# Vision block on one core: variances and gate logit in four 32-column tiles, roots and gate weights spread through DRAM

## What is computed

```python
h = tokens(x, W, b)                        # 196 patches + class token
h = h + attention(layernorm(h))            # 16 heads, "stablemax3" in place of softmax
h = h + experts(layernorm(h))

# layernorm: (x - mean) / sqrt(var + 1e-5) over the 256 channels of a token
# experts, per token:
u = sigmoid(x @ Wu + bu)                   # the gate logit, one number a token
k = clip(ceil(4 * u), 1, 4)
h = relu(x @ W1[e] + b1[e]);  y[e] = h @ W2[e] + b2[e]
out = sum over i = 1..4 of where(k >= i, u / i, 0) * y[(token + i - 1) % 4]
```

## Time and profile before

| | |
|---|---|
| median of 3 runs | 3939.52 us (3939.36 to 3940.41) |
| span of the profiled execution | 3943.7 us; this is all the time that the profile has for it |
| PE busy | 3883.3 us (98%), 30276 records |
| PE weight loads (beside PE) | 3412.1 us (87%) |
| DVE, POOL, ACT busy | 2816.3 (71%), 2819.3 (71%), 2380.1 us (60%) |
| DMA | 545.57 MB, mean 138 GB/s; SP's queue 46.7% of 16 engines |
| chain that ended last | PE 95% |

### The profile page before, as it was taken

How to read it: one execution, slowest core, us unless ns; L and a number is a source line. 1 busy time by engine, 2 the same in 40 slices (tenths; PEclk the granted TensorE clock), 3 DMA queues, 4 the chain that set the end, 5 groups by cost and what they waited for, 6 DMA issues and landing times.

```text
span 3943.7 us, 87143 instructions
## 1 busy us (share of the span) xinstructions
PE 3883.3 (98%) x30276; PEld 3412.1 (87%) x30276; DVE 2816.3 (71%) x4315; ACT 2380.1 (60%) x4388; POOL 2819.3 (71%) x3543
## 2 busy tenths in 40 slices
PE   7899999999999999999999999999999999999998
PEld 4688888888888888888888888888888888888887
DVE  5767777777777677777777777777777777777753
ACT  5655566655666655666555666556665556665552
POOL 5666777767777667777677776677776777766676
PEclk8999999999999999999999999999999999999999
DMA  7244444444444444444444444444444444444455
GB/s 237 91 138 142 123 145 140 134 139 139 127 142 137 141 139 126 141 140 134 141 137 129 144 136 139 137 129 138 142 135 143 136 129 141 137 138 125 136 148 140
DMA packets 776547, 545.57 MB, mean 138 GB/s; under 512 B 157624, under 2 KB 701752, under 8 KB 775096
## 3 DMA queue, kind: packets, MB, share of 16 engines
q1 hardware_dynamic: 771416, 539.70, 46.7%
q10 hardware_dynamic: 4704, 0.30, 0.1%
HBM read 518.48 MB, written 21.30 MB: 137 GB/s over the span
## 4 chain that ended last, share of the span: by engine, by line
PE 95%; POOL 1%; ACT 1%; DVE 1%; issue 1%; DMA 0%; ACTq 0%; SPq 0%; POOLq 0%; DVEq 0%
PE ps L1336 66%; PE ps L1420 5%; PE ps L1435 5%; PE ps L1449 5%; PE ps L1534 4%; PE ps L1543 3%; PE ps L1551 2%; PE ps L1518 1%; PE ps L1512 1%; PE ps L1332 1%; PE ps L1524 1%; PE ps L1500 1%; PE ps L1506 1%; ACT probs L712 0%; DVE lows L1046 0%
## 5 line engine op out<-in xcount | busy, mean ns | idle before, releaser
L1336 PE MATMUL ps<-xn,w1s 128*128 128x197 f32 x4096 | 910.1, 343 | 4.6 <-ACT hT L677 2.3
L1336 PEld LDWEIGHTS ps<-xn,w1s 128*128 128x128 f32 x4096 | 676.6, 189 | 144.0 <-issue 132.3
L1336 PE MATMUL ps<-hT,w_s 128*128 128x197 f32 x4064 | 783.8, 330 | 7.6 <-issue 7.3
L971 DVE SCALAR_TENSOR_TENSOR probs<-probs,ps 99x788 f32<-99x788 f32 x512 | 483.4, 970 | 323.4 <-ACT probs L712 323.4
L1336 PEld LDWEIGHTS ps<-hT,w_s 128*128 128x128 f32 x4064 | 691.7, 190 | 9.6 <-issue 7.9
L568 POOL TENSOR_TENSOR hT<-hT 128x197 f32<-128x197 f32 x508 | 331.4, 652 | 511.9 <-ACT hT L692 508.7
L1336 PE MATMUL ps<-xt,w1s 128*128 128x197 f32 x3072 | 681.8, 330 | 3.3 <-ACT hT L683 1.7
L561 POOL TENSOR_SCALAR hT<-hT 128x394 f32<-128x394 f32 x512 | 642.7, 1255 | 19.2 <-DVE hT L1092 19.2
L1046 DVE TENSOR_REDUCE lows<-ps 99x8 f32<-99x1576 f32 (+1 forms) x256 | 460.3, 1799 | 219.4 <-PE ps L1435 219.4
L1336 PE MATMUL ps<-hT,w_a 128*128 128x197 f32 x3048 | 591.0, 329 | 0.2 <-DVE yw L1110 0.2
L1336 PEld LDWEIGHTS ps<-xt,w1s 128*128 128x128 f32 x3072 | 539.1, 190 | 36.3 <-DVE hT L1098 3.4
(11 more groups left out here) (142 smaller groups left out, 6231.8 us busy)
## 6 DMA issues: line engine op xcount, KB each, us to landing
w_s<-w_sums SPq DMA_DIRECT2D x508, 256.0 KB, 3.6
w_a<-in_w SPq DMA_DIRECT2D x384, 256.0 KB, 3.3
w1s<-w_sums SPq DMA_DIRECT2D x512, 192.0 KB, 2.6
w1s<-in_w SPq DMA_DIRECT2D x512, 128.0 KB, 2.3
x<-in_xT SPq DMA_DIRECT2D x30, 1188.0 KB, 7.3
w1s<-in_w SPq DMA_DIRECT2D x512, 64.0 KB, 1.9
w1s<-w_sums SPq DMA_DIRECT2D x512, 64.0 KB, 1.9
out_rows<-rows SPq DMA_DIRECT2D x252, 48.0 KB
```

The source lines that it names most:

```text
L971: nc.vector.scalar_tensor_tensor(out=part, in0=part, scalar=3.75, in1=ps[0:HB, 2 * half:2 * half + 2, 0:N], op0=ALU.add, op1=ALU.mult).the ...
L1336: return mm(place, weights, rows, start=start, stop=True, skip_group_check=True)
```

## The change

`variance`, `variance2` and the gate logit are computed in four products each, with 32 weight columns and 100 of the tokens (QUARTERS starts at 0, 100, 197 and 297), each into its own 32 partitions of one bank. A partition group so holds a quarter of the tokens, and eps, roots, Newton step, sigmoid and gate weights are worked on 128 x 100 instead of 128 x 394. To have them on all partitions again, SP stores one partition of each group (4 x 100) to DRAM, waits, and reads it back to all 128 partitions: `spread_rstd`, `spread_rstd2` (200 KB read) and `spread_weights` (four experts, 800 KB read). The logit is summed from hc instead of xn2, inside `variance2`, and is multiplied by the root afterwards; `gate_product` and `gate_sum` move ahead, `gates` moves from s = 5 to s = 3, the variance of f half a unit later and into bank Y1.

```diff
+        QUARTERS = (0, QW, S, S + QW)
...
+            def spread_rstd(f):
+
+                sp.wait_ge(rstd_ready, at(f, 1, 1))
+                wait(sp, xn2_ready, at(f - 2, 1, 1))
+                sp.dma_start(rstd_rows, rstd_q[0:P:32, :]).then_inc(rstd_out, 16)
+                sp.wait_ge(rstd_out, at(f, 16, 16))
+                sp.dma_start(rstd[:], rstd_rows.rearrange("q x -> (q x)").partition_broadcast(P)).then_inc(rstd_in, 16)
...
+            def spread_weights(n):
+
+                sp.wait_ge(gate, at(n, GATES, GATES))
+                wait(sp, yw_ready, 2 * n * E)
+                sp.dma_start(weight_rows.rearrange("e q x -> q e x"), w_q[0:P:32, 0:E * QW].rearrange("q (e x) -> q e x", e=E)).then_inc(we_out, 16)
+                sp.wait_ge(we_out, at(n, 16, 16))
+                sp.dma_start(w_e[:], weight_rows.rearrange("e q x -> (e q x)").partition_broadcast(P)).then_inc(we_in, 16)
...
                 for s in range(16):
+                    if s == 4 and has_f and f > 1:
+                        spread_rstd(f)
+                    if s == 15 and has_b:
+                        spread_rstd2(b, has_f)
+                    if s == 5 and has_n:
+                        spread_weights(n)
...
             def gates(n):
 
-                pool.wait_ge(gate, at(n, 9, 3))
-                wait(pool, yw_ready, 2 * n * E)
+                pool.wait_ge(gate, at(n, GATES, 2))
+                wait(pool, we_in, at(n, 16, 0))
...
-                    if s == 5 and has_n:
+                    if s == 3 and has_n:
                         gates(n)
...
             def normal_rows2(b):
-                refine_1(b, rs2_ready, nt2_ready, ht2_ready)
-                refine_2(b, ht2_ready, rstd2_ready)
-                nc.vector.tensor_tensor(xn2[:, b % 2], hc[:], rstd[:].unsqueeze(1).broadcast_to((P, DK, N)), ALU.mult).then_inc(xn2_ready, 1)
+                dve.wait_ge(rstd2_in, at(b, 16, 16))
+                for kk in range(DK):
+                    ins = nc.vector.tensor_tensor(two(xn2[:, b % 2, kk, :]), two(hc[:, kk, :]), padded(rstd[:]), ALU.mult)
+                ins.then_inc(xn2_ready, 1)
...
-                mm(bank("var2", b)[:, 0:N], mean_w[:], xn2[:, b % 2, 0, :], start=True, stop=True).then_inc(var2_done, 1)
-
-            def gate_logit(b, *free):
+                squared = xn2[:, b % 2].rearrange("p k n -> p (k n)")
+                for i, first in enumerate(QUARTERS):
+                    ins = mm(quarters(i)[:, home("var2", b), 0:QW], mean_w[:, 32 * i:32 * i + 32], squared[:, first:first + QW], start=True, stop=True)
+                ins.then_inc(var2_done, 1)
                 pe.wait_ge(zs_ready, at(b, 1, 1))
-                for w in free:
-                    pe.wait_ge(*w)
-                mm(bank("z", b)[:, 0:N], ones[:], hc[:, 0, :], start=True, stop=True).then_inc(z_done, 1)
+                for i, first in enumerate(QUARTERS):
+                    ins = mm(quarters(i)[:, home("var2", b), QW:2 * QW], ones[:, 32 * i:32 * i + 32], zs[:, first:first + QW], start=True, stop=True)
+                ins.then_inc(z_done, 1)
```

More of the change, by code:

```diff
@@ L46, in vit_block @@
     GP = 200
+    QW = GP // 2
     UNITS = E * FB
@@ L96, in vit_block @@
         carrier = sb("carrier", [P, 1])
[L97 to L100, removed]
+        zs = sb("zs", [P, 2 * GP])
+        zb = sb("zb", [P, QW])
+        ez = sb("ez", [P, QW])
+        u = sb("u", [P, QW])
+        w_q = sb("w_q", [P, E * (QW + 1)])
+        w_e = sb("w_e", [P, E * 2 * GP])
         hT = sb("hT", [P, (RING * 2 + RING2 * 2 + RINGT * 3) * S])
@@ L467, in _ @@
                 nc.gpsimd.memset(tile[:], 1.0).then_inc(pool_const, 1)
-            for tile in (xn, q_max, k_one, lows, h2, zb):
+            for tile in (xn, q_max, k_one, lows, h2, zb, zs):
                 nc.gpsimd.memset(tile[:], 0.0).then_inc(pool_const, 1)
@@ L796, in ez_of @@
                 act.wait_ge(zb_ready, at(n, 1, 1))
-                wait(act, gate, at(n - 1, 9, 9))
+                wait(act, gate, at(n, GATES, 0))
                 nc.scalar.activation(ez[:], zb[:], ACT.Exp, scale=-1.0).then_inc(ez_ready, 1)
@@ L1115, in y_weighted @@
                     dve.wait_ge(d2_ready, x + 1)
-                    dve.wait_ge(gate, at(x // E, 9, 9))
+                    dve.wait_ge(we_in, at(x // E, 16, 16))
                 else:
@@ L1252, in step @@
                         odd_up(k)
+                    if k == 3 and has_f:
+                        refine_2(f, ht_ready, rstd_ready)
                     if has_b:
@@ L1291, in step @@
                     even(8 + k)
+                    if k == 7 and has_b:
+                        normal_rows2(b)
+                    if k == 6 and has_b:
+                        refine_1(b, rs2_ready, nt2_ready, ht2_ready)
+                        refine_2(b, ht2_ready, rstd2_ready)
                     if has_f:
                         low(f, k)
+                    if k == 6 and has_b:
+                        zb_of(b)
                     odd_up(8 + k)
@@ L1312, in step @@
                     if k == 5 and has_b:
+                        gate_sum(b)
+                        logits(b)
                         spread(b, "var2", var2_done, vt2_ready)
-                    if k == 6 and has_b:
-                        normal_rows2(b)
-                        gate_sum(b)
-                    if k == 7 and has_b:
-                        zb_of(b)
                     if k == 7 and has_f:
@@ L1684, in step @@
                 experts(1)
+                experts(1)
                 if has_f:
-                    variance(f, read(5))
-                experts(1)
+                    variance(f, (h_ready, at(f, 2, 2)))
                 if has_b:
-                    gap(b, 3, read(6), *([(vt_ready, at(f, 1, 1))] if has_f else []))
+                    gap(b, 3, read(6))
                 experts(1)
@@ L1694, in step @@
                 if has_b:
-                    weigh(b, 0)
+                    weigh(b, 0, *([(vt_ready, at(f, 1, 1))] if has_f else []))
                     gap(b, 4, read(8))
```

125 lines of the change are left out of this document (77 added, 48 removed).

## The result

The changed kernel takes **4080.8 us** (median of 4 runs, 4072.18 to 4088.23) against 3939.44 us: 1.0355 times as long, 95% interval 1.0342 to 1.0367. The prediction was 4005 with a range up to 4055. The sign was right; the size was 76 us short.

What follows compares the result with a forecast made beforehand. TensorE (PE) was taken as the bound, busy 120.38 of 120.42 us a step. Steady terms of +1.1 a step gave +33 us, the start +33: +66, median 4005 us, chance 0.50, range up to 4055.

Steps and rivals of the forecast that it cites:

- What PE saves: On PE, 0.35 us from the variance and 0.73 from variance 2 with logit: 1.1 a step, -33 us in all.
- Rival (c): On PE, the tiles do not run side by side: +0.5 a step in place of -1.1, 4053 us; chance 0.04.
- The variance moves half a unit back.: The variance of f goes to about 1952.9 on PE; only its root, expected at 1956.3, was then followed.
- The trip of a root, 4.8 us: Through DRAM by SP's queue: 2.1 for the store, 0.4 to issue the read, 2.3 for the 200 KB read.
- Root of f: At s = 4, xn is there at 1962.2, before PE wants it: covered with 0.8 us to spare, no stall.
- the two don't add: At s = 5, PE's stalls for SP's loads (1.1) and POOL's gates (1.0) overlap: +1.3 us a step, 0.5 to 2.8.
- normal_rows2 before low(f, 7), +0.7: On DVE at s = 15, two products delay the reduction PE's transposes need: +0.7 us a step, 0.3 to 1.0.
- Logit, +0.2: In the second normalization, PE waits for z, which needs DVE's gate_sum: +0.2 us a step, 0 to 0.6.
- The start, +33: In pair 0's step, DVE waits for pair 1's root, late in SP's queue: +33 us once, 27 to 36.
- Rival (b): At s = 5, the weight broadcast runs at 222 GB/s: stall 2.8, +2.6 us a step, 4050 us; chance 0.14.
- what the profile after would show: First steady step near 161, steady step 121.5 us, PE idle at named places, four variance records starting within 0.03 us.
- the two signs by which I would have been wrong: The start is not longer by over 25 us, or a steady step is under 120 us.

Runs made afterwards that it cites:

- all repairs: Changed kernel with SP's weight spread later, normal_rows2, gates and gate_sum earlier, variance of f back, first roots on ACT's queue, two 1 MB loads held: 3933.06 us.

## Why the prediction was wrong, point by point

*What bounds the kernel.* Right. What was added in front of PE in each step came out in full: 29 steps of 3.15 are 91.5 of the 131.5.

*What PE saves.* Predicted 1.1 a step. The variance saved 0.35, as said. The second block costs 0.70 without its wait (0.97 less 0.27) for 1.35: 0.65, where I had 0.73. Together 1.0. Rival (c) is out: the first four records of the variance start within 0.02 us (2034.85 to 2034.87), and the block takes 0.31 for 0.66. The switch costs 0.09 in and 0.10 out, measured in three places; the 175 ns of TensorE: Matmul & The Clock Gate in the Trainium skill (Single matmul latency) is not seen in them.

*"The variance moves half a unit back."* **The first failed step**, a term put at nothing. I costed the move at nothing and looked only at the root behind it. The product was cover for DVE's up_sums; removing it from there costs 0.48 a step, about 14 us. The earlier trace rows show the place; what they don't show, and what the argument needed, is that DVE's up_sums end only 0.33 us ahead of the product behind.

*The trip of a root, 4.8 us.* Right in the sum: 1.6 from the store to the issue of the read and 3.1 to its landing, 4.7 in the median and 4.9 in the step shown. The parts were not right, and that their errors cancel was luck: I had 2.5 (2.1 and 0.4) and 2.3. By DMA: Bandwidth & Descriptors in the Trainium skill (Anatomy of one DMA) the receipt of the last write is heaviest where the target is HBM. By that the store would take longer than a load of its size. That section is written for DMAs that GpSimd issues; these come from SP. The trace has no load of 1.6 KB on SP's queue to compare; the store took 1.61 with SP's wake-up, against 2.0 for loads of 64 KB, so nothing here shows a dearer store.

*Root of f, "covered, with 0.8 to spare".* xn was in time (2044.17 for a wish at 2044.82). But PE also waits for poly, which stands behind xn on DVE and ended at 2045.05. I had noted that poly comes later and did not follow it to PE: +0.24.

*s = 5, "the two don't add".* **The second failed step, and the largest: +1.3 became +2.3.** POOL's part, 1.0, was right (0.96). SP's chain was right in time: the store was foreseen 12.5 us behind `gap(b, 3)` (1965.7 less 1953.2) and came 12.7 behind it. Sized too low was the load stall, 1.1 for 1.8: the broadcast took 4.5 to land in place of 3.9, and in six steps 5.6 to 6.6, where SP's next issue took 1.0 to 1.6 us. And the two add in large part. Without POOL's stall the load's is 1.8 (1.33 and the 0.46 that came back there), without the load's POOL's is 0.91 (the kernel with `spread_weights` at s = 6); together they are 2.3, of the 2.7 that they would be if nothing were shared. I had let them share 0.8 of 2.1.

*normal_rows2 before low(f, 7), +0.7.* Right: 0.82. *Logit, +0.2.* Right: 0.27.

*The start, +33.* Right: 34.6, by the mechanism named. DVE's xn of pair 1 ended at 107.7, 36.8 later than before, where I had 34.5, and 2.2 of it came back, where I had 1.5. The earlier trace rows has two slices below the 222 GB/s that I called the slowest, 188 and 166; only the top of my range hangs on that.

So the sum was +66 in place of +131.5 of the span: 0.5 a step from unit 3, 1.0 from s = 5, 0.24 from poly, and some 0.3 from the small terms; the tail's 5.4 was not in it. Rival (b), the slow broadcast at 4050, had the right place; the broadcast's rate was only part of its cost. Of the rivals none had a cover that goes with the product moved.

Of "what the profile after would show", the start (a first steady step at 163.2 for about 161) and the places of waiting came true. The step of 121.5 did not: it is 123.6. Neither of the two signs by which I would have been wrong came up; neither looked for a step that is too long.

## What to carry to other kernels

Where an engine is busy all the time, a small product is also the cover of whatever is due just behind it. Before moving one, read for both places when the next instruction's inputs are ready, and look for what stands behind each waiting instruction, on its own queue too, that the bound engine needs. A blocking wait on the queue that issues the loads should stand behind the loads that are due next: here one turn of the loop was worth 48 us, more than all that the tiles could save.

## What was not expected of the hardware

A small DMA on another engine's queue was held up by those in flight. At 24.29 ACT's queue issued 1.6 KB; SP's last 1 MB load landed at 27.53, and ACT went on behind its store at 27.73, 3.4 after the issue. The kernel with all repairs shows that the loads were the cause: with two of the four held back, the same store at the same place took 1.64, as in the steady state:

```profile
22.74 1.05 ACTq L386 DMA_DIRECT2D rstd_rows<-rstd_q  x1
24.38 0.35 ACTq L388 DMA_DIRECT2D rstd<-rstd_rows  x1
```

The store of root 1, issued there beside the weight sums and a 1 MB load, took 4.1 in both kernels.

The issue itself can take long: behind the 800 KB broadcast (0.32) a 64 KB load took 1.45 us to issue in the changed kernel, where 0.43 is usual, and the broadcast of that step took 6.3 to land.

```profile
1552.05 0.32 SPq L449 DMA_DIRECT2D w_e<-weight_rows  x1
1552.41 1.45 SPq L407 DMA_DIRECT2D w1s<-in_w  x1
```

Why six steps went so and the others did not was not tried.
